# Two experts' feed-forward products put into the drain of an attention and mixture-of-experts kernel

## The chip, the cores and the metric

The kernel runs on one core of a Trainium2 chip. The metric is the device time of one execution in microseconds, and the time before is the median of three runs. TensorE (PE) does the matrix products, VectorE (DVE), ScalarE (ACT) and GpSimd (POOL) the work on vectors, and SyncE (SP) issues the transfers. The profile is of one execution.

## What is computed

The input is 32 batches of 128 tokens of 128 numbers. Two attention stages with modulated linear layers come first, each batch by itself; then a mixture of 8 experts over all 4096 tokens:

```
x = x + attn(cond(x))                       # 16 heads, softmax over tokens
tok = cond2(x)                              # 16 heads of 8, mixes heads of one token, then a linear layer
logits = tok @ gate_w.T ; probs = softmax(logits)
top2_w, top2_idx = top_k(probs, 2)
cap = int(1.25 * T / E)                     # 640
keep = (bincount(top2_idx) <= cap)          # an expert chosen more often is dropped whole
y[t, e] = relu(tok @ W1[e] + b1[e]) @ W2[e] + b2[e]
out = x + sum over e of (weight of e if chosen and kept) * y[t, e]
```

For the inputs of the reference the experts 0 to 7 are chosen 146, 280, 2077, 2615, 289, 1995, 572 and 218 times. Five of them (0, 1, 4, 6, 7) are at or below 640 and are kept. As first choices of the tokens of the first 24 batches they are chosen 20, 94, 928, 1247, 63, 521, 150 and 49 times.

## The kernel before

**The batch loop.** All engines walk through slots. Slot s works on batch s + 1 (queries, keys, values; stage A), s (scores and attention; B), s - 1 (output product, first residual, keys of the mixing stage; C), s - 2 (scores and softmax between heads; H) and s - 3 (the mixing sum and the last linear layer, whose result is one batch of `tok_all`; D). Slots -2 to 34 exist. From slot 32 (BATCH) on no attention is left: this is the drain. Each engine's order is the order in the text of its block; semaphores carry the dependences. In slots 33 and 34 `late(s)` puts the head scores first on DVE. The mixing sum of a batch is a product with the weights and a tree of adds: the first half of the shifts on DVE (`mix_lo`, L343 to L360), the other on POOL (`mix_hi`, L1056 and L1063); `mixed()` joins them. POOL also makes `pair` (L1068), the products from which DVE takes the head scores (L377); `score` is then completed by two copies on ACT (`head_copies`), and `weight` is the exponential on ACT (`head_weights`).

**Routing.** `gate_logits` on PE multiplies tiles of `tok_all` with the gate matrix. The tiles 0 to 27 (EARLY) come in six parts in slots 31 to 33 and one copy, the last four (RECENT) at the end. `first_choice` and `second_choice` on DVE pick the two best experts of each tile; then the count over all tokens (L434, a product with ones on PE, L753), `keep`, the gates, and a ranking that gives `order`, the kept experts first, and `n_run`, their number (L448 to L460). `step` makes each of these instructions wait for the one before. `keep_going(n)` on PE is n products of ones with no use for the result.

**The expert loop.** For each of the `n_run` experts, 8 quads of 4 tiles (512 tokens): `hidden` (L779, one product of 128x128 by 512 columns), `relu` on ACT into `hT`, `output` (L787, four products), and on DVE four instructions (L482) that add the result times the gate to `acc_all`. Each product in 32 bits appears in the profile as two instructions, so `hidden` is x2 and `output` x8. `acc_all` begins as the transposed x (`x1_transpose` on PE, `copy_x1` on ACT), to which the second bias is added (`bias_rows` L771 on PE, L470 on DVE). At an expert's start ACT loads its number from `order` and copies its weights (`set_expert`, `set_hidden`). In the last round SP writes each quad of `acc_all` out as it is done.

## Time and profile before

| | us |
|---|---|
| median of 3 runs (594.38 to 597.33) | 596.59 |
| profiled execution, its time | 596.94 |
| its span, first to last instruction | 595.1 |
| PE busy in the span | 575.1 (97%) |
| DVE busy | 483.7 (81%) |
| ACT busy | 372.0 (63%) |
| POOL busy | 288.1 (48%) |

Times inside the profile are microseconds from the span's start; 1.84 us of the execution lie outside its span. A busy PE is not a PE at its peak, since the ends of matmuls are modelled. The batch loop fills the span up to about 471 us, the drain and the routing go up to about 518 us, and the expert loop to the end.

### The profile page before, as it was taken

How to read it: one execution, taken by the hardware profiler on the slowest of the kernel's cores; microseconds unless marked ns; L12 is line 12 of the kernel's file. 1: busy time of each engine (PE TensorE's matmuls, PEld its weight loads, DVE VectorE, ACT ScalarE, POOL GpSimd, SP SyncE). 2: the span in 40 equal slices, each digit the busy share in tenths (PEclk: the TensorE clock that was granted, in tenths of full speed). 3: DMA queues.
4: the chain of work that ended last, by engine and by line, in shares of the span. 5: the costliest groups of instructions: out<-in, count | busy, mean ns of one | idle time of the engine just before them, and what ended most of it. 6: DMA issues, size and time to landing. Idle time of an engine off the chain costs nothing. (4 is left out here: it accounts for less than half of the span.)

```text
span 595.1 us, 15251 instructions
## 1 busy us (share of the span) xinstructions
PE 575.1 (97%) x4516; PEld 492.3 (83%) x4516; DVE 483.7 (81%) x1026; ACT 372.0 (63%) x855; POOL 288.1 (48%) x248
## 2 busy tenths in 40 slices
PE   8999999999999999999999999999998997799998
PEld 8888888888888888888888888888887896466775
DVE  4235888898989898988889898989898788777776
ACT  1767767777777677777777767777775321534443
POOL 1011666666666666666666666666666563000000
PEclk9999999999999999999999999999999977999999
DMA  7300000000000000000000000000000000000004
GB/s 240 86 2 2 1 3 2 0 0 0 0 0 0 0 0 0 0 0 0 0 0 0 0 0 0 0 0 0 0 0 2 1 1 0 1 1 0 0 0 141
DMA packets 9364, 7.18 MB, mean 12 GB/s; under 512 B 1089, under 2 KB 8833, under 8 KB 9217
## 3 DMA queue, kind: packets, MB, share of 16 engines
q1 hardware_dynamic: 9344, 6.94, 3.9%
q8 instruction: 11, 0.18, 0.1%
q14 instruction: 9, 0.07, 0.0%
HBM read 4.84 MB, written 2.10 MB: 12 GB/s over the span
## 5 line engine op out<-in xcount | busy, mean ns | idle before, releaser
L1068 POOL TENSOR_TENSOR pair<-kx 128x1152 f32<-128x1152 f32 x32 | 82.2, 2568 | 167.4 <-DVE shifted L388 158.4
L580 PE MATMUL bank_a<-v,prob 128*128 128x65 f32 x1024 | 128.5, 274 | 1.5 <-ACT prob L814 0.8
L580 PEld LDWEIGHTS bank_a<-v,prob 128*128 128x128 f32 x1024 | 121.8, 192 | 6.3 <-ACT prob L814 3.2
L1063 POOL TENSOR_TENSOR mix_hi<-mix_hi 128x512 f32<-128x512 f32 (+2 forms) x96 | 116.8, 1217 | 7.5
L271 DVE TENSOR_REDUCE row_max<-bank_s 128x4 bf16<-128x512 f32 x128 | 88.9, 694 | 26.2 <-PE bank_s L555 25.3
L814 ACT ACTIVATE prob<-bank_t 128x512 f32<-128x512 f32 x128 | 68.9, 589 | 6.9 <-PE bank_t L570 4.7
L587 PE MATMUL misc<-yT,wq_sb 128*128 128x128 f32 x512 | 69.6, 279 | 0.5 <-DVE yT L419 0.5
L570 PE MATMUL bank_t<-qT,kT 64*128 64x256 f32 x512 | 65.7, 376 | 0.0
L1056 POOL TENSOR_TENSOR mix_hi<-weight,kx 128x1024 f32<-128x1024 f32 x32 | 64.1, 2002 | 3.1 <-ACT weight L814 3.1
L282 DVE TENSOR_TENSOR att<-bank_a,recip_den 128x256 f32<-128x256 f32 x128 | 54.4, 425 | 13.0
L587 PEld LDWEIGHTS misc<-yT,wq_sb 128*128 128x128 f32 x512 | 62.0, 191 | 3.6 <-DVE yT L419 0.7
L814 ACT ACTIVATE attT<-misc 128x512 f32<-128x512 f32 x64 | 38.1, 595 | 42.1 <-PE misc L594 42.1
L660 PE MATMUL misc<-attT,wpost_sb 128*128 128x128 f32 x512 | 64.1, 278 | 0.0
L660 PEld LDWEIGHTS misc<-attT,wpost_sb 128*128 128x128 f32 x512 | 59.7, 192 | 0.0
L814 ACT ACTIVATE hT<-bank_t,b_now 128x512 f32<-128x512 f32 x42 | 28.9, 687 | 42.7 <-PE bank_t L779 42.6
L570 PEld LDWEIGHTS bank_t<-qT,kT 64*128 64x128 f32 x512 | 49.3, 189 | 4.9
L349 DVE TENSOR_TENSOR mix_lo<-mix_lo 128x512 f32<-128x512 f32 x32 | 52.4, 1637 | 1.1
L814 ACT ACTIVATE qT<-misc 128x512 f32<-128x512 f32 x64 | 38.0, 594 | 23.0 <-PE misc L587 23.0
L555 PE MATMUL bank_s<-k,q 128*128 128x256 bf16 x256 | 49.8, 276 | 1.9 <-ACT k L814 0.3
L343 DVE TENSOR_TENSOR mix_lo<-weight,kx 128x1024 f32<-128x1024 f32 x32 | 49.9, 1560 | 0.0
L779 PE MATMUL bank_t<-tok_all,w_now 128*128 (+1 forms) x84 | 42.1, 595 | 1.6 <-ACT w_now L814 1.6
L377 DVE TENSOR_REDUCE score<-pair 128x144 f32<-128x1152 f32 x32 | 43.1, 1346 | 0.0
(149 smaller groups left out, 998.9 us busy)
## 6 DMA issues: line engine op xcount, KB each, us to landing
...
b_rows<-in_b SPq DMA_DIRECT2D x16, 4.0 KB
```

The costliest lines, as they stand in the source:

```text
L271: V.tensor_reduce(bass.AP(row_max, first_w * (P + 1) + HPG * p, [[HPG * P, P], [P + 1, 2], [KEY, 2], [1, 1]]), bank_s[:, :, :].rearrange(" ...
L282: V.tensor_tensor(att[:, HPG * g:HPG * (g + 1), :], att_bank(g)[:, :, 0:KEY], recip_den[:, g % 2, :].unsqueeze(2).to_broadcast([P, HPG, KEY]),
L343: V.tensor_tensor(mix_lo[:, :, :].rearrange("p r (h e) -> p r h e", e=MD), weight[:, jd, 0:MH // 2, :].unsqueeze(3).to_broadcast([P, MH // ...
L349: V.tensor_tensor(mix_lo[:, 0:4, :], mix_lo[:, 0:4, :], mix_lo[:, 4:8, :], ALU.add).then_inc(s_lo, 1)
L570: last = mm(bank_t[half][:, w:w + 2, :], kT[rows, j, p, :], qT[rows, j, p, w:w + 2, :], start=False, stop=True, skip_group_check=True)
L580: last = mm(att_bank(g)[:, w, :], prob[:, g % 2, w, :], v1[:, j, g, :], start=(w == 0), stop=True, skip_group_check=True)
L587: last = mm(bank[:, c % 4, :], wq_sb[:, c * P:(c + 1) * P], yT[:, :], start=(c % 4 == 0), stop=True, skip_group_check=True)
L660: last = mm(misc[2][:, 0, :], wpost_sb[:, k, :], attT[:, k, :], start=(k == 0), stop=(k == CHUNKS - 1))
L814: return nc.scalar.activation(out_, in_, func, **kw)
L1056: G.tensor_tensor(mix_hi[:, :, :].rearrange("p r (h e) -> p r h e", e=MD), weight[:, jd, MH // 2:MH, :].unsqueeze(3).to_broadcast([P, MH / ...
L1063: G.tensor_tensor(mix_hi[:, 0:r, :], mix_hi[:, 0:r, :], mix_hi[:, r:2 * r, :], ALU.add).then_inc(s_hi, 1)
L1068: G.tensor_tensor(pair[:, :, :], bass.AP(kx2, jc * 2 * P, [[4 * P, P], [0, SHIFTS], [1, P]]), bass.AP(kx2, jc * 2 * P, [[4 * P, P], [MD, S ...
```

## The change

Two experts are computed ahead, in the drain, before it is known how many are kept. The first choices of the tokens of 24 batches are counted (`count_ahead`, with one product of ones on PE), and the two least chosen experts (`pick_ahead`) go into `ahead_order`. Their 16 units (an expert and a quad each) of `hidden`, `relu`, `output` and a copy to `ahead_out` (`ahead_keep`) are laid into slots 32 to 34 and behind them on PE and ACT, in place of most of `keep_going`; `unit` puts quad 7, which needs the last tokens, last. The loop then runs over the kept experts without these two (`not_ahead`, `keep_loop`), at least three times. With the counts above the two are experts 0 and 7, and 1, 4 and 6 are left. `ahead_out` is scaled with the gates and added to `acc_all` during the loop: 48 tiles are scaled by ACT, three behind each `relu` of the first two experts (`scale_three`), 16 by POOL, which also does all adding.

The other edits: the 24 early tiles' logits come in four parts in slot 31; the last eight are RECENT, and `second_choice` runs once over all 32. In the drain DVE makes the copies of `score` itself (`own_copies`), and the tree of adds of `mix_lo` is one strided reduction into `mix_part`. `mix_hi` has two buffers. The ranking for the loop goes ahead of the scaling of the gates. The transposes of x come behind the units, and the second half of them, the transposes of the gates and the bias products behind the first `hidden` products; the bias is added within the first expert. The loops of the first two experts are written out.

```
+AHEAD = 2
+EARLY, RECENT = range(BATCH - 2 * QUAD), range(BATCH - 2 * QUAD, BATCH)
...
+        UNITS = AHEAD * QUADS
+        HALF = QUADS // 2
+        SCALED = [(x, t) for q in range(QUADS) for x in range(1 if q < HALF else AHEAD)
+                  for t in range(q * QUAD, (q + 1) * QUAD)]
...
+            def ranked(into):
...
+            def count_ahead():
+
+                dve.wait_ge(s_log_mm, 4)
+                dve.wait_ge(s_const, 3)
+                top, fi = part(r_max, EARLY), part(first, EARLY)
+                lg = misc[0][:, :, :].rearrange("p w f -> p (w f)")[:, 0:len(EARLY) * EXPERTS].rearrange(
+                    "p (t e) -> p t e", e=EXPERTS)
+                step(V.tensor_reduce(top, lg, AX.X, ALU.max))
+                ROUTE_STEPS["tops"] = step(V.tensor_tensor(fi, lg, over_e(top), ALU.is_ge))
+                ROUTE_STEPS["count1"] = step(V.tensor_reduce(count[:, :], fi.rearrange("p t e -> p e t"), AX.X, ALU.add))
...
+            def pick_ahead():
+
+                dve.wait_ge(s_cnt1_mm, 1)
+                step(V.scalar_tensor_tensor(out=key[:, :], in0=bank_s[:, 0, 0:EXPERTS], scalar=float(EXPERTS),
+                                            in1=index8[:, :], op0=ALU.mult, op1=ALU.add))
+                ROUTE_STEPS["pick"] = ranked(ahead_order)
+                step(V.tensor_scalar(not_ahead[:, :], place[:, :], float(AHEAD), None, ALU.is_ge))
...
+                def drain_slot():
+                    def weight_sums():
+                        dve.wait_ge(s_weight, n(d))
+                        need(dve, s_mix, n(d - 1))
...
+                    if s == BATCH:
+                        count_ahead()
+                        weight_sums()
+                        pick_ahead()
...
+                    head_scores()
+                    own_copies()
+                    head_shift()
...
+                        V.tensor_reduce(mix_part[:, :], mix_lo[:, :, :].rearrange("p r f -> p f r"), AX.X,
+                                        ALU.add).then_inc(s_lo, 3)
+                        mixed(mix_part[:, :])
...
-            second_choice(RECENT, 2)
+            second_choice(range(BATCH), 2)
...
+            step(V.tensor_tensor(keep_loop[:, :], keep[:, :], not_ahead[:, :], ALU.mult))
+            step(V.scalar_tensor_tensor(out=key[:, :], in0=keep_loop[:, :], scalar=-float(EXPERTS), in1=index8[:, :],
+                                        op0=ALU.mult, op1=ALU.add))
+            ROUTE_STEPS["order"] = ranked(order)
...
+            ROUTE_STEPS["loop"] = step(V.tensor_tensor(loop_gates[:, :, :], gates[:, :, :], over_t(not_ahead), ALU.mult))
...
+            for q in range(QUADS):
+                dve.wait_ge(s_x1n, q + 1)
+                add_expert(0, q)
+                for done in ((q,) if q < HALF else (2 * q - 8, 2 * q - 7) if q >= QUADS - 2 else ()):
+                    add_b2(done)
             dve.wait_ge(s_b2, QUADS)
-            with dve.Fori(0, runs) as k:
+            for q in range(QUADS):
+                if q < HALF:
+                    dve.wait_ge(s_added, q + 1)
+                add_expert(1, q)
+            with dve.Fori(2, runs) as k:
...
-            early_ends = (0, 6, 10, 15, 20, 24, len(EARLY))
-            parts_early = [EARLY[a:b] for a, b in zip(early_ends, early_ends[1:])]
+            parts_early = [EARLY[a:b] for a, b in ((0, 6), (6, 13), (13, 19), (19, 24))]
...
+            def ahead_hidden(u):
+
+                x, q = unit(u)
+                need(pe, s_ah, u - 1)
+                if q == QUADS - 1:
+                    pe.wait_ge(s_tok, BATCH)
+                pe.wait_ge(s_ah_w1, x + 1)
+                mm(bank_t[u % 2][:, :, :], ahead_w1[:, x, :], tok_all[:, q * QUAD * P:(q + 1) * QUAD * P],
+                   start=True, stop=True).then_inc(s_ah_mm, 1)
+
+            def ahead_output(u):
+
+                x, q = unit(u)
+                pe.wait_ge(s_ah, u + 1)
+                need(pe, s_ao, u - 1)
+                for t in range(QUAD):
+                    last = mm(bank_a[u % 2][:, t * P:(t + 1) * P], hT[:, u % 2, t * P:(t + 1) * P],
+                              w2_sb[:, bass.ds(picked[x], 1), :].rearrange("p a f -> p (a f)"),
+                              start=(t == 0), stop=True, skip_group_check=True)
+                last.then_inc(s_ao_mm, 1)
...
+            def ahead(*units):
+
+                for u in units:
+                    ahead_output(u)
+                    if u + 2 < UNITS:
+                        ahead_hidden(u + 2)
...
+                if s_is(s, BATCH - 1):
+                    gate_logits(parts_early[0])
...
+                    keep_going(6)
+                    pick()
+                    pe.wait_ge(s_ld_ffn, 16 * (3 + P // EXPERTS))
+                    ahead_hidden(0)
...
+                    if s_is(s, BATCH):
+                        ahead(0, 1, 2)
                     if s_is(s, BATCH + 1):
-                        keep_going(40)
+                        ahead(4, 5, 6)
                     if s_is(s, BATCH + 2):
-                        keep_going(12)
+                        ahead(8)
+                        gate_logits(RECENT[:-1])
                     need(pe, s_tok, d)
                     pe.wait_ge(s_mix, n(d))
                     nc.tensor.transpose(misc[2][:, 0, :], mix[:, :], ident[:, :]).then_inc(s_mixT_mm, 1)
                 if s_is(s, BATCH):
-                    gate_logits(parts_early[5])
+                    ahead(3)
+                if s_is(s, BATCH + 1):
+                    ahead(7)
+                if s_is(s, BATCH + 2):
+                    ahead_output(9)
...
-            x1_transpose(range(QUADS // 2, QUADS))
+            ahead(12, 13, 14, 15)
+            x1_transpose(range(HALF))
...
+            x1_transpose(range(HALF, QUADS))
+            pe.wait_ge(s_rt, ROUTE_STEPS["gates"])
+            pe.wait_ge(s_x1n, QUADS)
+            for i in range(2):
+                src = gates[:, i * 16:(i + 1) * 16, :].rearrange("p t e -> p (t e)")
+                last = nc.tensor.transpose(misc[1][:, i, :], src, ident[:, :])
+            last.then_inc(s_gT_mm, 1)
+            for q in range(QUADS):
+                output(0, q, q % 2)
+                if q + 2 < QUADS:
+                    hidden(q + 2, q % 2)
+                if q == 0:
+                    pe.wait_ge(s_gT, 1)
+                    bias_rows(range(HALF))
+                if q == 5:
+                    bias_rows(range(HALF, QUADS))
...
+                def drain_slot():
+                    if s == BATCH:
+                        copy_att(c, 0)
+                        copy_att(c, 1)
+                        copy_logits(EARLY, 4)
+                        act.wait_ge(s_ld_ffn, 16 * (3 + P // EXPERTS))
+                        act.wait_ge(s_rt, ROUTE_STEPS["pick"])
+                        take_expert(0)
+                        x1_scaled()
+                        take_expert(1)
+                        ahead_relu(0)
+                        keys_out()
+                        ahead_relu(1)
+                        keys_twice()
+                        head_weights()
+                        ahead(0, 1, 2)
+                        mixing_out()
+                        ahead(3)
+                        tokens_out()
+                    if s == BATCH + 1:
+                        ahead(4)
+                        head_weights()
+                        ahead(5, 6)
+                        mixing_out()
+                        ahead(7)
+                        tokens_out()
+                    if s == BATCH + 2:
+                        ahead(8)
+                        mixing_out()
+                        ahead_keep(9)
+                        tokens_out()
+                        ahead_relu(11)
+                        copy_logits(RECENT, 6)
+                        route_exp(EARLY)
+                        route_exp(RECENT)
+                        ahead(10, 11)
...
+            def scale_three(i):
+
+                for x, t in SCALED[3 * i:3 * i + 3]:
+                    f(ahead_out[:, x, t, :], ahead_out[:, x, t, :],
+                      scale=ahead_gate[:, x, t:t + 1]).then_inc(s_scaled, 1)
...
+            for k in range(2):
+                e = next_expert(k)
+                for q in range(2, QUADS + 2):
+                    if q == QUADS:
+                        next_hidden(k, e)
+                    relu(k * QUADS + q + 1, q % 2)
+                    scale_three(k * QUADS + q - 2)
...
+            pool.wait_ge(s_ah_gate, AHEAD)
+            pool.wait_ge(s_ao, UNITS)
+            for q in range(QUADS):
+                quad = slice(q * QUAD, (q + 1) * QUAD)
+                own = q < HALF
+                if own:
+                    G.tensor_tensor(ahead_out[:, 1, quad, :], ahead_out[:, 1, quad, :],
+                                    ahead_gate[:, 1, quad].unsqueeze(2).to_broadcast([P, QUAD, P]),
+                                    ALU.mult).then_inc(s_pool_step, 1)
+                    pool.wait_ge(s_pool_step, 2 * q + 1)
+                pool.wait_ge(s_scaled, scaled_by(q))
+                G.tensor_tensor(ahead_out[:, 0, quad, :], ahead_out[:, 0, quad, :], ahead_out[:, 1, quad, :],
+                                ALU.add).then_inc(s_pool_step, 1)
+                pool.wait_ge(s_pool_step, 2 * q + 2 if own else HALF + q + 1)
+                pool.wait_ge(s_b2, q + 1)
+                pool.wait_ge(s_e, (2 if own else 2 + QUADS) * QUAD + QUAD * (q + 1))
+                G.tensor_tensor(acc_all[:, quad, :], acc_all[:, quad, :], ahead_out[:, 0, quad, :],
+                                ALU.add).then_inc(s_added, 1)
...
```

PE in the drain, from the last key transpose of slot 32 on. Before, slots 32 and 33, where L704 and L720 are the two products that end a batch's mixing stage and L526 is `keep_going`:

```order
L704 MATMUL misc2<-ident,mix 128x128
L610 MATMUL bank_s<-gate_sb,tok_all 128x8 x4
L720 MATMUL misc2<-mixT,modw_sb 128x128
L526 MATMUL bank_a1<-ones 128x128 x40
L704 MATMUL misc2<-ident,mix 128x128
L526 MATMUL bank_a1<-ones 128x128 x3
L720 MATMUL misc2<-mixT,modw_sb 128x128
```

And now, where L763 is `ahead_output`, L754 `ahead_hidden`, and L865 the former L704:

```order
L754 MATMUL bank_t1<-tok_all,ahead_w1 128x512
L852 MATMUL misc1<-ident,kxT 128x128
L763 ISA
L763 MATMUL bank_a0<-w2_sb,hT 128x128 x4
L754 MATMUL bank_t0<-tok_all,ahead_w1 128x512
L763 MATMUL bank_a1<-w2_sb,hT 128x128 x4
L754 MATMUL bank_t1<-tok_all,ahead_w1 128x512
L763 MATMUL bank_a0<-w2_sb,hT 128x128 x4
L754 MATMUL bank_t0<-tok_all,ahead_w1 128x512
L865 MATMUL misc2<-ident,mix 128x128
L763 MATMUL bank_a1<-w2_sb,hT 128x128 x4
L754 MATMUL bank_t1<-tok_all,ahead_w1 128x512
```

The filling products behind slot 32 are gone, and units stand ahead of and between the two products of each mixing stage.

PE behind the count of all tokens. Before:

```order
L753 MATMUL misc0<-count,ones 128x8
L621 MATMUL bank_t0<-ident,x_all 128x128 x4
L621 MATMUL bank_t1<-ident,x_all 128x128 x4
L621 MATMUL bank_a0<-ident,x_all 128x128 x4
L621 MATMUL bank_a1<-ident,x_all 128x128 x4
L759 MATMUL misc1<-ident,gates 128x128 x2
L771 MATMUL bank_a0<-b2_rows,gatesT 128x512
L771 MATMUL bank_a1<-b2_rows,gatesT 128x512
```

And now, where L916 is the count, L736 the transposes of x and L946 the load of `n_run` that stands ahead of the loop's first `hidden`:

```order
L916 MATMUL misc0<-count,ones 128x8
L763 MATMUL bank_a0<-w2_sb,hT 128x128 x4
L754 MATMUL bank_t0<-tok_all,ahead_w1 128x512
L763 MATMUL bank_a1<-w2_sb,hT 128x128 x4
L754 MATMUL bank_t1<-tok_all,ahead_w1 128x512
L763 MATMUL bank_a0<-w2_sb,hT 128x128 x4
L763 MATMUL bank_a1<-w2_sb,hT 128x128 x4
L736 MATMUL bank_a0<-ident,x_all 128x128 x4
L736 MATMUL bank_a1<-ident,x_all 128x128 x4
L736 MATMUL misc1<-ident,x_all 128x128 x4
L736 MATMUL bank_a0<-ident,x_all 128x128 x4
L946 TENSOR_LOAD n_run
```

Units 12 to 15 now stand between the count and the transposes of x, and the transposes ahead of the first `hidden` of the loop.

## Rows read from the trace of the kernel before

**Rows 1.** Page, costliest groups: relu of the loop.
```profile
L814 ACT ACTIVATE hT<-bank_t,b_now 128x512 f32<-128x512 f32 x42 | 28.9, 687 | 42.7 <-PE bank_t L779 42.6
```
**Rows 2.** Timeline, expert loop: start, duration, engine, line, out<-in, idle before.
```profile
518.09 1.16 PE L787 MATMUL bank_s<-w_run,hT 128*128 x8
...
526.32 1.05 PE L787 MATMUL bank_s<-w_run,hT 128*128 x8
...
527.80 1.30 DVE L482 SCALAR_TENSOR_TENSOR acc_all<-bank_s,gate_run,acc_all 128x128 f32 x4 [0.53 <-PE bank_s L787]
...
533.83 1.15 PE L787 MATMUL bank_s<-w_run,hT 128*128 x8
...
577.66 1.15 PE L787 MATMUL bank_s<-w_run,hT 128*128 x8
```
**Rows 3.** Timeline, slot 31, PE's waits and a part of the logits.
```profile
456.35 0.63 PE L594 MATMUL misc<-ident,att 128*128 128x128 f32 x4 [0.61 <-DVE att L282]
...
458.05 0.40 PE L652 MATMUL bank_s<-ident,row_max 128*128 128x128 bf16 x4 [0.79 <-DVE row_max L271]
...
460.12 1.40 PE L610 MATMUL bank_s<-gate_sb,tok_all 128*128 128x8 f32 x12
```
**Rows 4.** Windows of 3 us in the drain: busy time by engine, then granted clock.
```profile
474.00:477.00 3.00, 2.05 (x20) 1.96 (x19) 2.93 (x6) 0.40 (x1) 2.84 (x3) 1.00 0.00 0
...
480.00:483.00 3.00, 3.00 (x16) 3.00 (x16) 2.41 (x4) 1.17 (x4) 1.73 (x1) 0.50 0.00 0
...
492.00:495.00 3.00, 0.97 (x7) 0.81 (x7) 2.85 (x5) 0.42 (x1) 1.96 (x1) 1.00 0.00 0
```
**Rows 5.** Timeline, drain: DVE's share of the mixing, and what follows it.
```profile
482.11 2.81 DVE L343 TENSOR_TENSOR mix_lo<-weight,kx 128x1024 f32<-128x1024 f32 x1
...
489.36 1.34 DVE L377 TENSOR_REDUCE score<-pair 128x144 f32<-128x1152 f32 x1
...
492.48 0.42 ACT L814 ACTIVATE weight<-shifted 128x256 f32<-128x256 f32 x1 [1.11 <-DVE shifted L388]
...
497.93 1.21 DVE L343 TENSOR_TENSOR mix_lo<-weight,kx 128x1024 f32<-128x1024 f32 x1
...
504.15 0.46 ACT L814 ACTIVATE tok_all<-misc,modb_sb,demod 128x128 f32<-128x128 f32 x1 [0.58 <-PE misc L720]
```
**Rows 6.** Timeline, routing: transposes, copies, count, ranking, bias.
```profile
505.81 1.04 PE L621 MATMUL bank_a<-ident,x_all 128*128 128x128 f32 x8
...
506.92 1.09 ACT L814 ACTIVATE acc_all<-bank_a 128x512 f32<-128x512 f32 x2
...
508.07 0.61 DVE L434 TENSOR_REDUCE count<-chosen 128x8 f32<-128x256 f32 x1
...
511.14 0.17 DVE L448 SCALAR_TENSOR_TENSOR key<-keep,index 128x8 f32<-128x8 f32 x1
...
512.11 0.70 PE L771 MATMUL bank_a<-b_rows,gatesT 32*128 32x512 f32 x2 [0.51 <-ACT gatesT L814]
...
513.22 0.15 DVE L460 TENSOR_SCALAR n_run<-kept 128x1 int32<-128x1 f32 x1
...
514.33 0.20 ACT L814 ACTIVATE b_now<-b_sb 128x1 f32 x1 [2.28 <-DVE n_run L460]
...
514.50 1.28 DVE L470 TENSOR_TENSOR acc_all<-acc_all,bank_a 128x512 f32<-128x512 f32 x2 [0.90 <-issue]
```
**Rows 7.** Groups by shape, POOL from 494 to 498 us: a sum of 512.
```profile
L1063 POOL TENSOR_TENSOR mix_hi<-mix_hi 128x512 f32<-128x512 f32 x1 | 1.3, 1292 | 0.1
```
**Rows 8.** Groups by shape, whole span: the same sum, and ACT scaling one tile.
```profile
L1063 POOL TENSOR_TENSOR mix_hi<-mix_hi 128x512 f32<-128x512 f32 x32 | 67.1, 2096 | 2.5
...
L814 ACT ACTIVATE x1s<-x_all,style 128x128 f32 x26 | 10.4, 402 | 30.8 <-DVE x_all L353 30.8
```
**Rows 9.** Timeline, slot 31: POOL's sums and a DVE addition from PSUM.
```profile
457.90 4.07 POOL L1063 TENSOR_TENSOR mix_hi<-mix_hi 128x512 f32<-128x512 f32 x3
...
460.72 0.28 DVE L353 TENSOR_TENSOR x_all<-misc,x_all 128x128 f32<-128x128 f32 x1
```

416 lines of the change are left out of this document (250 added, 166 removed).

## The prediction

> **What bounds the kernel now.** I read the page first: relu runs 42 times [rows 1]. Two of these stand ahead of the expert loop and eight are in each round, so the loop has (42 - 2) / 8 = 5 rounds, as many as there are kept experts. Then the timeline of the loop. The first output product starts at 518.09 and that of the second expert at 533.83, a first round of 15.74 us; by the row at 577.66 the next three take (577.66 - 533.83) / 3 = 14.61 us each [rows 2]. PE sets this pace: a quad takes 14.61 / 8 = 1.83 us, and in it DVE works 1.30 us, then waits for PE, and ACT 0.69 us [rows 1, 2]. So five rounds are 15.74 + 4 x 14.61 = 74.2 us, up to 592.3, and 2.8 us follow.
>
> The stretch from about 471 to 518.09 is the other half of the matter. Here the engines take turns: the share of PE's time in use was 0.97 of 3 us in the window at 492, and its clock fell to the lower level, 1.2 GHz (granted 0.50), in that at 480, soon after a window (474) with 2.05 of 3 us busy [rows 4]. What sets the time there is a chain by way of DVE and POOL: head scores, weights of the last batch (492.48), mixing sum, its tokens (done 504.61), then the routing on DVE up to `n_run` (513.37) and ACT's load of the first expert's number (514.33) [rows 5, 6]. PE has room there, filled with products of ones.
>
> **Rounds taken out.** The two experts picked are 0 and 7 by the counts, both kept, so the loop makes max(3, 3) = 3 rounds. Two rounds go: -29.2 us. The rest of the sum is what this costs.
>
> **Slot 31.** All 24 early tiles' logits now stand here; 6 tiles take 1.40 us, 0.23 us each [rows 3]. Six of them enter where PE waited 0.61 us, +0.8; seven where it waited 0.79 us for `row_max`, +0.8; six stand where six stood, and five instead of four make 0.2. Behind those waits everything of the slot follows, so I count it whole: +1.7 us. Slot 32 loses its 18 tiles, but there PE had waits.
>
> **Slot 32.** DVE no longer starts with the sum of weights and products; it counts first (three steps, about 1.4 us), ranks (the same chain as from 511.14 to 513.37, 2.2 us [rows 6]) and only then adds x. Before, that addition was as late for another reason: the sums in `mix_lo` ran against POOL. So it stays near its time. The pick is ready about 4 us into the slot's DVE work; PE and ACT each load two numbers, for which the row at 514.33 gives about 1 us from the number to the first copy [rows 6]. These delay the key products by 1.2 us on PE and `kx` by 1.6 on ACT. Who waits: POOL's `pair` of batch 31. Before, it waited for `shifted` of batch 30 until 481.27; now `shifted` comes at about 478.9 (no mixing ahead of it) and `kx` at 480.4, so `pair` starts 0.8 us earlier than before. The first `ahead_output` starts at about 479.8.
>
> **The mixing sum.** The three adds of `mix_lo` become one reduction. The nearest row below is the reduction of 1152 numbers, 1.34 us, read in another order; a reduction with a stride took 0.61 us for 256, which for 1024 gives 1.9 us at most by proportion above a fixed 0.15 [rows 5, 6]. I take 1.5. What it gives is mainly a place free of POOL: the product ahead of it took 2.81 us beside POOL and 1.21 us alone [rows 5]. The Trainium skill (SBUF — State Buffer, section "Who interferes with whom") says that a DVE reduction never contends with GpSimd, while a DVE instruction with two SBUF inputs does; the two rows of the product agree, and by it the reduction would cost its own time only. With head scores first in every slot, batch 31 goes so: `pair` 2.6 us from 480.4, the reduction 1.34, its copies, maximum and shift some 1.7, so shifted at 486.1; ACT takes it behind unit 6's relu, its weights at 490.4 (before 492.90). POOL's product and three sums (about 2.0 and 2.7 us, the largest sum 1.29 [rows 7]) and the join follow, some waits between them, and the sum of batch 31 is ready at about 497.3.
>
> **The drain by PE.** From 479.8 to the tokens of batch 31 PE has ten outputs and nine hiddens ahead of them, 9.5 x 1.83 = 17.4 us, seven tiles of logits 1.7, five small products of the mixing 1.9, and then the last product's hop over ACT, PE and ACT, 1.5: 502.3. The mixing sum at 497.3 is earlier than PE gets to it, so PE is the bound here, and its clock counts. The trace had the lower level for about 7 us from 478 on behind such a half-filled slot 32 [rows 4]; slot 32 is filled no better now. Work of 3 us is lost if it comes again; I take 2.5. With slot 31 the tokens are at 502.3 + 1.7 + 2.5 = 506.5, 1.9 later than the 504.61 of before.
>
> **Routing.** From tokens to the end of the count it was 508.68 - 504.61 = 4.1 us [rows 5, 6]. Now `second_choice` is 256 wide instead of 32, seven steps at about 0.45 instead of 0.22, +1.6, and the copy of the logits stands behind a relu, +0.7: 6.3 us, so 512.8. The product over it 0.5: 513.3. PE has idled some 2.5 us by then. Ranking comes 2 us earlier after the count than before, but nobody waits for that now: PE first does units 12 to 15, four outputs and two hiddens, 5.7 us: 519.0. The last copy 0.7; then four quads of transposes (0.52 each) and, slower, their copies on ACT (0.55 each [rows 6]), 2.7: 522.4. ACT loads the number and copies `w1`, 0.8; two hiddens 1.9: 525.1; the other four quads with their copies 3.0; the transposes of the gates 0.5. The loop's first output is at **528.6, against 518.09: +10.5 us**.
>
> **The three rounds.** The first holds eight bias products in two lots. One takes 0.70 us [rows 6]; four side by side use different rows of the array, and I take 1.2 a lot (0.7 to 2.8): +2.4. DVE has 8 x 1.30 and 8 x 0.64 (from the row of two at 514.50 [rows 6]), 15.5 us, less than the round. ACT has a relu of 0.69 and three tiles to scale: 0.40 us each alone [rows 8], less back to back, as two copies in 1.09 show; 0.8 to 1.2 for three against the 1.83 of a quad. So 0 to 0.1 us a quad, and I take 0.5 us a round for the borders, where ACT also loads and copies weights. POOL makes 20 sums of 512, 1.29 us each by the nearest row [rows 7]: 26 us of the 32 in two rounds, and each quad of the first four (3.9 us) is due only in the second round. Hidden. Rounds: 14.6 + 2.4 + 0.5 = 17.5, 15.1, 14.6: 47.2 us. End of the loop 575.8, the same 2.8 us of tail: span 578.6.
>
> **The sum.** Span before 595.1, now 578.6, -16.5. With the 1.84 us outside the span, 580.4 against the profiled 596.94; the median is 0.35 lower, so **580 us**.
>
> **Rivals.**
> - The clock stays up in the drain, since units take the place of waits: no 2.5 us, and scaling on ACT costs nothing, 1.0 less: 576.5. For: PE is filled from 479.8 on. Against: what came before the fall at 478 stays. 20%.
> - The clock falls twice, the second time in the 2.5 us of idle ahead of the count, as after the window at 492: another 3.5 us of lost work, 583.5 to 587 where slot 32 takes longer too. 17%.
> - POOL is late. Beside DVE its sum took 2.10 us in the mean of 32 [rows 8]. A first quad is then 6.4 us, four 25.7, and the fourth is due at the second round's fourth quad, 17.5 + 5.5 = 23 us in: DVE waits about 3, and again somewhat in the third round: 584. 8%.
> - Slower: DVE's additions in the loop (L482) share POOL's port and wait out each sum. The row at 460.72 speaks against it: an addition from PSUM took its 0.28 us in the midst of POOL's sums [rows 9]. But L482 also reads a gate from SBUF. If each of 20 sums at 1.29 to 2.10 us holds DVE, its 20.8 + 5.1 us in two rounds become 52 to 68 instead of 32.6: 599 to 615. It decides from about 1.2 us lost a sum. 4%. The Trainium skill's same section lets a DVE instruction with one SBUF input outside the fast modes pass POOL; by that the price is zero.
> - The change doesn't do what it says: a picked expert is not kept. With one, four rounds, 594.6; the counts (146 and 218 against 640) exclude it but for an error of mine. 1%.
>
> My forecast has 50%. The range takes in both clock cases, the late POOL, and the bounds above: 574 to 588. About 0.5% is what a measurement can tell from no change: faster 0.94, same 0.02, slower 0.04.
>
> **What would show it.** relu of the loop 26 times, and 16 units; first output of the loop near 528.6; three rounds of 17.5, 15.1 and 14.6 us; `mix_part` at 1.2 to 1.9 us whatever POOL does; L482 at its 0.33 us a tile beside POOL's sums; POOL ready before the third round. A window at granted 0.50 after 478 would show the clock term. Wrong would be a first output after 535 or DVE waiting for `added`.

## The result and the profile after

| | before | after |
|---|---|---|
| median, us | 596.57 (594.38 to 597.33, 4 runs) | 577.02 (574.82 to 579.19, 4 runs) |
| ratio to before | | 0.9678, 95% interval 0.9622 to 0.9734 |
| profiled execution, its time | 596.94 | 579.19 |
| its span | 595.1 | 577.4 |

The change takes off 19.6 us. The page of after gives the busy time of each engine, and the chain by engine:

```profile
PE 559.4 (97%) x4408; PEld 475.4 (82%) x4408; DVE 457.8 (79%) x966; ACT 390.7 (68%) x911; POOL 310.5 (54%) x268
...
PE 81%; DVE 8%; ACT 5%; issue 3%; DVEq 1%; POOL 0%; ACTq 0%; POOLq 0%
```

PE is as full as before, 97%, with 15.7 us less to do. The loop now has three rounds, as the output products that begin them show, in the timeline of PE (start, duration, then engine, line and operation):

```profile
527.30 1.06 PE L939 MATMUL bank_s<-w_run,hT 128*128 128x128 f32 x8
...
544.18 1.15 PE L939 MATMUL bank_s<-w_run,hT 128*128 x8 [0.17 <-DVE acc_all L569]
...
559.05 1.15 PE L939 MATMUL bank_s<-w_run,hT 128*128 x8 [0.17 <-issue]
```

The first round begins at 527.30, where it was 518.09 [rows 2]: 9.2 us later. The rounds take 16.88 and 14.87 us, and 18.35 go from the third round's start to the end of the span. Between slot 32 and the loop this is what stands at the places the sum spoke of, in the timeline of all engines:

```profile
478.41 0.31 ACT L985 ACTIVATE ahead_w<-w_sb 128x128 f32 x1 [3.48 <-DVE not_ahead L384]
...
481.43 0.33 PE L852 MATMUL misc<-ident,kxT 128*128 128x128 f32 x1
481.65 1.15 PE L763 MATMUL bank_a<-w_sb,hT 128*128 x8
482.17 1.92 DVE L514 TENSOR_REDUCE mix_part<-mix_lo 128x128 f32<-128x1024 f32 x1
...
484.17 0.38 ACT L985 ACTIVATE kx<-misc 128x256 f32<-128x256 f32 x1 [2.16 <-DVE mix_part L514]
...
484.63 2.59 POOL L1346 TENSOR_TENSOR pair<-kx 128x1152 f32<-128x1152 f32 x1 [7.73 <-ACT kx L985]
...
485.98 1.16 PE L763 MATMUL bank_a<-w_sb,hT 128*128 x8 [0.56 <-ACT hT L985]
...
492.46 0.41 ACT L985 ACTIVATE weight<-shifted 128x256 f32<-128x256 f32 x1
...
495.15 1.25 DVE L398 TENSOR_TENSOR mix<-mix_sum,h_rden 128x128 f32<-128x128 f32 x1
...
496.55 0.30 PE L865 MATMUL misc<-ident,mix 128*128 128x128 f32 x1 [1.21 <-DVE mix L398]
...
503.98 0.45 ACT L985 ACTIVATE tok_all<-misc,modb_sb,demod 128x128 f32<-128x128 f32 x1
...
509.96 0.61 DVE L533 TENSOR_REDUCE count<-chosen 128x8 f32<-128x256 f32 x1
...
510.72 0.36 PE L916 MATMUL misc<-count,ones 128*128 128x8 f32 x2 [2.24 <-DVE count L533]
...
519.06 1.06 PE L736 MATMUL bank_a<-ident,x_all 128*128 128x128 f32 x8 [0.78 <-ACT ahead_out L985]
```

Two things in it are not as in the sum. ACT's copy `kx` of batch 31 waits 2.16 us for DVE's `mix_part` of batch 29, a wait for the buffer: `kx2` has two halves, and batch 31 is to be written to the one of batch 29. What reads that half is DVE's product, and it was done at 482.07; but the copy's wait counts up to the end of the reduction behind it (484.09), which reads only `mix_lo`. And unlike before [rows 4], the clock falls not in the drain's middle but at its two ends, as the windows show (busy time of PE, PEld, DVE, ACT and POOL, then the granted clock):

```profile
465.00:468.00 3.00, 3.00 (x26) 2.74 (x27) 1.22 (x4) 0.67 (x3) 0.00 (x0) 0.88 0.00 0
468.00:471.00 3.00, 3.00 (x15) 1.92 (x13) 1.01 (x2) 1.78 (x6) 1.29 (x1) 0.55 0.02 5
...
480.00:483.00 3.00, 2.85 (x15) 1.74 (x14) 2.86 (x4) 1.67 (x3) 0.00 (x0) 1.00 0.00 0
...
507.00:510.00 3.00, 1.48 (x8) 0.65 (x6) 2.76 (x8) 1.74 (x3) 0.00 (x0) 1.00 0.00 0
510.00:513.00 3.00, 2.28 (x12) 1.79 (x12) 2.57 (x10) 0.60 (x1) 0.00 (x0) 0.78 0.00 0
513.00:516.00 3.00, 3.00 (x12) 2.19 (x11) 2.69 (x10) 1.16 (x2) 0.00 (x0) 0.66 0.00 0
```

The second fall follows the 2.24 us in which PE waits for the count, as one of the rivals had it. The first stands at the end of slot 31, behind windows in which PE was busy (2.73 of 3 us at 462, 3.00 before).

### The profile page after: what moved, and what is told of

Same layout as the page of the kernel before. It is cut to its first block, busy times and chain, and to the rows that moved or that the text cites. A ratio compares the mean times of both kernels' runs of the same rounds, so it can differ in the third digit from the quotient of the medians.

```text
span 577.4 us, 14607 instructions
## 1 busy us (share of the span) xinstructions
PE 559.4 (97%) x4408; PEld 475.4 (82%) x4408; DVE 457.8 (79%) x966; ACT 390.7 (68%) x911; POOL 310.5 (54%) x268
## 4 chain that ended last, share of the span: by engine, by line
PE 81%; DVE 8%; ACT 5%; issue 3%; DVEq 1%; POOL 0%; ACTq 0%; POOLq 0%
PE bank_a L692 18%; PE misc L699 10%; PE misc L815 10%; PE bank_t L682 8%; PE bank_s L667 6%; PE misc L706 5%; PE misc L833 3%; PE bank_t L677 3%; PE bank_t L931 3%; PE misc L835 2%; DVE row_max L296 2%; DVE h_max L412 2%; PE bank_s L939 2%; PE misc L939 2%; PE bank_s L807 1%
## 5 line engine op out<-in xcount | busy, mean ns | idle before, releaser
L450 DVE TENSOR_TENSOR mix_lo<-mix_lo 128x512 f32<-128x512 f32 x29 | 47.2, 1627 | 1.0
L444 DVE TENSOR_TENSOR mix_lo<-weight,kx 128x1024 f32<-128x1024 f32 x29 | 43.8, 1511 | 0.0
L985 ACT ACTIVATE q<-qT 128x512 bf16<-128x512 f32 x64 | 40.3, 630 | 1.1
L706 PE MATMUL misc<-ident,att 128*128 128x128 f32 x256 | 39.2, 276 | 0.5 <-DVE att L307 0.5
```

The source lines that it names most:

```text
L706: last = nc.tensor.transpose(misc[1 + half][:, c % 4, :], att[:, 2 * c:2 * c + 2, :].rearrange("p h e -> p (h e)"), ident[:, :])
L985: return nc.scalar.activation(out_, in_, func, **kw)
```

## The experiments

Each is compared with the kernel before on its own chip, and changes the kernel after unless said otherwise. The changed kernel again, the last units first, the keys' own buffer and the tree ran on one chip (before: 598.18 us). So did, later, the long filling and the two runs with the count product between the units (598.23). Nothing combined, one expert ahead, both together and the drain's order alone ran on a second (598.29), the shorter filling on a third (597.9). Between chips it is the ratio to before that can be compared. The theory at the start: the two rounds out are worth what a round takes, and the rest is PE's chain through the drain, in which a wait for `kx`, the strided sum, the place of the last four units and the combining each have a price of their own. The rivals: units are nearly free, or the drain's new order on DVE and ACT brings a good part of it.

**The changed kernel again.**

> The changed kernel again, as the base of the others on the same chip. My theory of its spread (575.0 to 579.2 us in four runs): TensorE's clock falls to its lower level once or twice around the drain, and each fall costs 1 to 2 us, so runs lie in two groups. The rival, a spread of the batch loop itself, would show in the time at which slot 32 begins. Expected: median 575 to 579 us, and in the profile one or two stretches with a granted clock near 0.5 to 0.7.

578.23 us (577.35 to 583.32), ratio 0.9686 (0.9656 to 0.9715). In this profile the clock did not fall anywhere between 450 and 531, so the one or two stretches expected there did not come; its fall stands at 9 to 15 us (granted 0.83 and 0.60). The first output came at 525.97, and the two rounds took 16.89 and 14.86 us. The time does go with the mean granted clock. Of the ten executions of this kernel two at 1.0 took 574.8 and 575.0 us, four at 0.996 to 0.997 577.4 to 578.2, three at 0.993 579.0 to 579.3, and one at 0.985 583.3.

The rival, a spread of the batch loop, is half right. From the first transposes of `att` to those of slot 31 the fourteen profiles, that of before too, take 421.4 to 421.6 us: the loop is steady. But the first ones start anywhere from 31.06 to 34.17 us. Up to 3 us between two profiles thus stand ahead of everything that an edit has touched, so two profiles are compared below from slot 31 or from a later common place. What makes the start differ was not followed.

The repeated run is the yardstick for what follows, and for slot 31. The first transposes of `att` in that slot stand at 455.48 (454.92 before), and the second ones of slot 32 at 473.00:

```profile
455.48 0.60 PE L706 MATMUL misc<-ident,att 128*128 128x128 f32 x4
...
473.00 0.63 PE L706 MATMUL misc<-ident,att 128*128 128x128 f32 x4 [0.45 <-DVE att L307]
```

Before, they were at 471.28. The lag grows from 0.56 to 1.72 us, so all of slot 31's new logits cost 1.2 us.

**The last units ahead of the count.**

```
             pe.wait_ge(s_log, 2)
+            ahead(12, 13, 14, 15)
             pe.wait_ge(s_rt, ROUTE_STEPS["count"])
             mm(misc[0][:, 0, 0:EXPERTS], ones[:, :], count[:, :], start=True, stop=True).then_inc(s_cnt_mm, 1)
-            ahead(12, 13, 14, 15)
             x1_transpose(range(HALF))
```

> Units 12 to 15 stand ahead of the count of all tokens instead of behind it. Theory: behind the drain PE is the bound, and it idles 2.2 us ahead of the count and then has 5.3 us of units in front of the transposes; taken first, the units fill the idle time, and the ranking, later by about 3 us, is still ready when ACT has copied the transposes: 2 to 3.5 us faster than the changed kernel, the loop's first output near 524.5. Rival: the ranking on DVE and ACT's load of the expert's number set the start of the loop; then the count's delay of 3.3 us goes straight through and it is 1 to 3 us slower.

574.97 us (573.83 to 575.35), ratio 0.9604 (0.9587 to 0.9622): 3.3 us less than the changed kernel by the medians, with intervals that do not overlap. From the tokens of batch 31 to the first output the profile has 19.06 us (504.41 to 523.47), against 21.66 in the repeated run (504.31 to 525.97): 2.6 us. In PE's timeline the wait for the count is gone, and the one for the first weights stays (1.24 us, 1.15 in the repeated run):

```profile
512.25 2.10 PE L763 MATMUL bank_a<-w_sb,hT 128*128 x16
514.19 0.29 PE L917 MATMUL misc<-count,ones 128*128 128x8 f32 x2
515.13 1.07 PE L736 MATMUL bank_a<-ident,x_all 128*128 128x128 f32 x8 [0.66 <-ACT ahead_out L985]
...
518.34 1.98 PE L931 MATMUL bank_t<-tok_all,w_now 128*128 128x512 f32 x4 [1.24 <-ACT w_now L985]
```

From 504 to 513 its windows hold 3.00 of 3 us of PE at granted 1.00. So the place of the four units was wrong by some 3 us: work that does not need the count stood behind the wait for it.

**A buffer of its own for the keys of batch 31.**

```
-        kx2 = sb("kx2", [P, 2, 2 * P])
+        kx2 = sb("kx2", [P, 3, 2 * P])
...
+                kc, kd = (2 if s_is(c, BATCH - 1) else jc), (2 if s_is(d, BATCH - 1) else jd)
...
-                    need(act, s_lo, 4 * n(c - 2))
-                    need(act, s_hi, 4 * n(c - 2))
-                    f(kx2[:, jc, :].rearrange("p (r f) -> p r f", r=2),
+                    if kc != 2:
+                        need(act, s_lo, 4 * n(c - 2))
+                        need(act, s_hi, 4 * n(c - 2))
+                    f(kx2[:, kc, :].rearrange("p (r f) -> p r f", r=2),
```

> The last batch's keys (kx) get a buffer of their own, so that ACT's copy of them in slot 32 no longer waits for the mixing of batch 29 on DVE (2.2 us). Theory: this wait, which I had not seen, also holds ACT's relu of unit 2 and PE behind it, and POOL's pair; without it the copy comes at about 482.0 instead of 484.2, PE's waits ahead of units 2 and 5 (1.4 and 2.0 us) shrink, and the last tokens come 1 to 2 us earlier: 1 to 2 us faster. Rival: the mixing of batches 30 and 31 on DVE is the bound of the drain, which does not start earlier: within 0.5 us of the changed kernel.

577.35 us (576.88 to 577.60), ratio 0.9652 (0.9635 to 0.9668). That is 0.9 us less than the repeated run by the medians, but the intervals of the ratios overlap.

```profile
453.21 0.61 PE L707 MATMUL misc<-ident,att 128*128 128x128 f32 x4
...
480.67 0.38 ACT L986 ACTIVATE kx<-misc 128x256 f32<-128x256 f32 x1
...
481.12 2.59 POOL L1350 TENSOR_TENSOR pair<-kx 128x1152 f32<-128x1152 f32 x1 [5.47 <-ACT kx L986]
...
502.21 0.45 ACT L986 ACTIVATE tok_all<-misc,modb_sb,demod 128x128 f32<-128x128 f32 x1
...
508.95 0.36 PE L917 MATMUL misc<-count,ones 128*128 128x8 f32 x2 [2.24 <-DVE count L534]
```

`kx` waits for nothing, and `pair` starts at 481.12. The tokens of batch 31 begin at 502.21 against 504.31 in the repeated run, but 2.1 us is not what the buffer gives. This execution was already 2.27 us ahead at the start of slot 31 (453.21 against 455.48). From there its tokens take 49.00 us. The repeated run, whose clock did not fall on the way, takes 48.83, and the first profile of the changed kernel, whose clock fell near the same place as here (granted 0.59 and 0.84 at 465 and 468), takes 49.34 (454.64 to 503.98). Against its like the buffer is worth 0.3 us at the tokens, and 0.4 at the loop's first output (72.25 against 72.66 us from slot 31). PE waits the same 2.24 us for the count, and here too the clock falls behind it (window in the same columns as above):

```profile
510.00:513.00 3.00, 3.00 (x10) 1.97 (x10) 2.60 (x12) 1.28 (x2) 0.00 (x0) 0.50 0.00 0
```

So the wait for the key buffer is real, and hardly anything hangs on it: what goes is PE's wait of 0.56 us ahead of unit 2, while the one of 1.2 us for `mix` stays (1.22 at 494.78). That is the rival's case, within 0.5 us, and not the theory's 1 to 2.

**The tree of adds instead of the strided reduction.**

```
-                        V.tensor_reduce(mix_part[:, :], mix_lo[:, :, :].rearrange("p r f -> p f r"), AX.X,
-                                        ALU.add).then_inc(s_lo, 3)
-                        mixed(mix_part[:, :])
+                        for i, r in enumerate((4, 2, 1)):
+                            V.tensor_tensor(mix_lo[:, 0:r, :], mix_lo[:, 0:r, :], mix_lo[:, r:2 * r, :],
+                                            ALU.add).then_inc(s_lo, 1)
+                            if r > 1:
+                                dve.wait_ge(s_lo, 4 * d + i + 2)
+                        mixed(mix_lo[:, 0, :])
```

> In the drain the strided reduction of mix_lo is again the tree of three adds. The reduction measures 1.92 to 1.96 us, the tree alone 0.69 + 0.38 + 0.29 = 1.36 us, but up to 4.4 us beside POOL. Theory: in slots 33 and 34 the tree runs beside POOL's product and sums, is longer by 0 to 2 us in each, and holds POOL's sums up as well: 0 to 2 us slower, at the last tokens. Rival: as the two now take turns otherwise, the tree is 0.6 us shorter in each slot, up to 1.5 us faster.

581.87 us (580.10 to 582.83), ratio 0.9722 (0.9703 to 0.9740): 3.6 us more, beyond both the theory (0 to 2) and the rival. The three adds of slot 32, of slot 33 and what followed them:

```profile
482.84 1.48 DVE L515 TENSOR_TENSOR mix_lo<-mix_lo 128x512 f32<-128x512 f32 x3
...
492.94 4.20 DVE L515 TENSOR_TENSOR mix_lo<-mix_lo 128x512 f32<-128x512 f32 x3
...
498.62 0.30 PE L868 MATMUL misc<-ident,mix 128*128 128x128 f32 x1 [3.04 <-DVE mix L398]
```

Alone the tree takes 1.48 us, less than the 1.92 of the reduction. Beside POOL's product and sums (493.18 to 498.32) it takes 4.20, where the reduction took 1.96 beside the product, PE waits 3.04 us instead of 1.21, and behind that the clock is at 0.64 and 0.79 in the windows of 498 and 501. The reduction in slot 33 is what decides; in slots 32 and 34 the tree is 0.4 us quicker (1.48 us in both). How the 3.6 us divide between the longer wait and the clock behind it is not shown.

**Nothing combined.**

```
-                    scale_three(k * QUADS + q - 2)
...
-                if q < HALF:
-                    dve.wait_ge(s_added, q + 1)
...
-                        dve.wait_ge(s_added, q + i + 1)
...
-            for q in range(QUADS):
-                quad = slice(q * QUAD, (q + 1) * QUAD)
...
-                G.tensor_tensor(acc_all[:, quad, :], acc_all[:, quad, :], ahead_out[:, 0, quad, :],
-                                ALU.add).then_inc(s_added, 1)
```

> The results of the two experts computed ahead are neither scaled (48 tiles on ACT, 16 on POOL) nor added (POOL's 16 sums) to the output; all else stays, so their part is missing from what comes out. Theory: the combining lies beside PE's work and costs only where ACT's scaling and its loads meet at the border of an expert: 0 to 1.5 us faster than the changed kernel (577 to 578 us). Rival: POOL's sums hold DVE's additions or the loop waits for them: 4 us faster or more, and DVE's 0.28 us a tile would fall.

This kernel leaves the two experts' part out of its output. 576.74 us (574.22 to 579.70), ratio 0.9662 (0.9641 to 0.9683), some 1.5 us less than the changed kernel, on another chip and with intervals that overlap. In the profiles the first two rounds take 16.88 and 14.67 us (16.88 and 14.87 after). The difference lies in the last round, DVE's timeline there:

```profile
563.60 1.30 DVE L591 SCALAR_TENSOR_TENSOR acc_all<-bank_s,gate_run,acc_all 128x128 f32 x4 [0.73 <-issue]
564.98 1.30 DVE L591 SCALAR_TENSOR_TENSOR acc_all<-misc,gate_run,acc_all 128x128 f32 x4
```

and the same two quads of after, where DVE waits for `added` ahead of each quad:

```profile
564.67 1.30 DVE L594 SCALAR_TENSOR_TENSOR acc_all<-bank_s,gate_run,acc_all 128x128 f32 x4 [0.71 <-issue]
566.13 1.42 DVE L594 SCALAR_TENSOR_TENSOR acc_all<-misc,gate_run,acc_all 128x128 f32 x4 [0.16 <-issue]
```

With the combining two quads take DVE 3.57 us (564.67 to 568.24), without it 3.41 (563.60 to 567.01), and PE needs 3.50. So with it DVE sets the pace of the last round: from the round's first output to DVE's last addition it is 15.62 us after, 15.06 without combining, 14.76 before. The run takes out the wait instruction, ACT's scaling and POOL's sums together, so it does not show which of them costs the 0.16 us.

**One expert ahead.**

```
-AHEAD = 2
+AHEAD = 1
...
-                        ahead(4, 5, 6)
+                        ahead(4)
+                        ahead_output(5)
+                        ahead_output(6)
+                        pe.wait_ge(s_ao, 7)
+                        keep_going(12)
                     if s_is(s, BATCH + 2):
-                        ahead(8)
+                        keep_going(12)
                         gate_logits(RECENT[:-1])
...
-            ahead(12, 13, 14, 15)
```

> Only one expert (0) is computed ahead: 8 units instead of 16, the loop has four rounds, some products of ones fill PE where units were. Theory: a round costs 14.6 us in the loop; in the drain the last four units behind the count cost 5.3 us with the 0.8 us wait for their last copy, the others lie beside the chain by way of DVE and cost up to 2 us. So one expert ahead is 14.6 - 6 to 8 = 7 to 9 us slower than two, 584 to 587 us, and the first expert alone is worth 11 to 14 us. Rival 1: units in the drain are free: 13 us or more slower than two (590 us or more). Rival 2: PE is the bound all through the drain: each unit costs its 1.75 us and one is as good as two (577 to 580 us).

591.33 us (589.73 to 591.40), ratio 0.9884 (0.9867 to 0.9901). The second expert is worth 13.1 us by the medians (11.8 by the ratios, since the repeated run has one execution of 583.32), nearly its whole round of 14.6. By this run alone its units are nearly free, as the first rival had it. But the tokens of batch 31 begin at 503.86 here and at 504.31 with 16 units (49.1 and 48.8 us from the start of slot 31), and the windows behind them are unlike:

```profile
504.00:507.00 3.00, 2.03 (x5) 1.11 (x5) 0.00 (x0) 1.20 (x4) 0.00 (x0) 0.63 0.00 0
507.00:510.00 3.00, 1.94 (x8) 1.64 (x8) 2.70 (x9) 1.03 (x3) 0.00 (x0) 0.50 0.00 0
510.00:513.00 3.00, 0.72 (x4) 0.76 (x5) 2.46 (x7) 0.00 (x0) 0.00 (x0) 0.50 0.00 0
```

PE waits 3.34 us for the count and is at the lower clock up to 522; the first four `hidden` instructions of the loop take 3.78 us instead of 1.98. Were the units free, or did they keep up the clock? Two more runs asked that.

**One expert ahead, PE's waits filled.** On top of the edit for one expert; `fill(n)` is `keep_going(n)` into a bank that nobody reads.

```
+                if s_is(s, BATCH + 1) or s_is(s, BATCH + 2):
+                    fill(5)
                 if D:
                     pe.wait_ge(s_mixT, n(d))
...
                 if s_is(s, BATCH + 2):
+                    fill(6)
                     ahead_hidden(7)
                     gate_logits(RECENT[-1:])
+                    fill(5)
                     ahead_output(7)
+                    fill(32)
```

> One expert ahead, as in the run with one, but PE's idle places in slots 33 and 34 and ahead of the count product are filled with products of ones into a bank that nothing reads (5 + 5 + 6 + 5 + 32 of them). In the run with one expert (591.33) PE idled 3.34 us ahead of the count product and its granted clock was 0.50 to 0.63 from 504 to 522. Theory: a good part of the 13 us between one and two experts ahead is the clock, which the units of the second expert keep up; with the filling it stays at 1.00 up to the loop, the four hidden and transposed tiles there go at full speed, and the time is 587.5 to 589.5. Rival: the units are simply nearly free places for 14.6 us of loop, and the clock's part is small: 590.5 to 592, as before, or more where the filling delays the count product.

592.02 us (591.66 to 593.56), ratio 0.9908 (0.9880 to 0.9935). The clock stayed at 1.00 from 471 to 531, and the time is no better, since the filling was too long:

```profile
509.11 7.31 PE L643 MATMUL bank_s<-ones 128*128 128x128 f32 x64
```

The 32 products took 7.31 us, up to 516.4, with the count ready at 513.1 (512.47 and 0.62). A product takes 7.31 / 32 = 0.23 us. By itself the run settles nothing. So once more, with 2, 2, 3, 2 and 16 products:

**One expert ahead, filled less.**

> As the filled run with one expert ahead (592.02), with less filling: 2, 2, 3, 2 and 16 products of ones instead of 5, 5, 6, 5 and 32. There the clock stayed at 1.00 and the first output came 5.4 us behind the first weights of the loop, against 7.4 in the run with one expert and no filling; but the filling, 7.31 us for the 32, held the count product about 3.3 us, and the tokens about 1. Theory: without that delay the clock's part is seen by itself: the first output of the loop 2 to 3 us earlier than 524.57, the time 588 to 590 against 591.33. Rival: the clock's part is nothing on the whole, since the low clock falls on stretches in which PE waits for DVE and ACT anyway: 590.5 to 592.

587.55 us (586.31 to 589.36), ratio 0.9834 (0.9812 to 0.9857): 3.8 us less than without filling by the medians, from 25 products whose result nobody reads. The two ran on different chips; the ratios to before differ by 3.0 us, with an interval of some 1.3 to 4.7.

```profile
508.06 3.74 PE L643 MATMUL bank_s<-ones 128*128 128x128 f32 x32
512.47 0.36 PE L926 MATMUL misc<-count,ones 128*128 128x8 f32 x2 [0.67 <-DVE count L533]
516.72 1.99 PE L940 MATMUL bank_t<-tok_all,w_now 128*128 128x512 f32 x4 [2.06 <-ACT w_now L994]
```

The granted clock is 1.00 from 474 to the loop. The first output comes at 521.77 against 524.57, 2.8 us earlier, though the tokens are 0.8 later, as this execution's start was. From tokens to first output it is 17.14 us against 20.71: 3.6 us. Since the filling does no work, this rules out that the low clock costs nothing. Against one expert with PE kept busy, the second is worth 587.55 - 578.23 = 9.3 us by the medians, and 10.4 by the profiles, from the first transposes of `att` to the end (552.5 and 542.1 us). So its eight units cost some 4 to 5 us of the 14.6, and 3 to 4 of the 13.1 are the clock, which the units keep up.

**The count ahead and the third buffer together.**

```
+            ahead(12, 13, 14, 15)
             pe.wait_ge(s_rt, ROUTE_STEPS["count"])
...
+        kx2 = sb("kx2", [P, 3, 2 * P])
```

> The keys' own buffer and the units ahead of the count together. Theory: the two gains add, since the tokens come about 2 us earlier (measured with the buffer alone, where a fall of the clock ahead of the count took half of it back) and no idle time is left ahead of the count: 5 us faster than the changed kernel, about 572 to 573 us. Rival: with the units ahead of the count ACT's load or the gates become the bound, and it is no faster than the units ahead alone, 575 us.

574.66 us (574.52 to 579.63), ratio 0.9614 (0.9599 to 0.9628): no better than the units first alone, 574.97 (0.9604), as the rival said. The third buffer adds nothing, which fits the 0.3 to 0.4 us read above.

**The count product between the units.** It stands behind unit 13, ahead of 14:

```
             pe.wait_ge(s_log, 2)
+            ahead(12, 13)
             pe.wait_ge(s_rt, ROUTE_STEPS["count"])
             mm(misc[0][:, 0, 0:EXPERTS], ones[:, :], count[:, :], start=True, stop=True).then_inc(s_cnt_mm, 1)
-            ahead(12, 13, 14, 15)
+            ahead(14, 15)
```

> The count product stands between unit 13 and unit 14 on PE, instead of ahead of 12 or behind 15. In the run with the units first (574.97) the count was ready at about 510.5, PE reached its product at about 513.3, and PE later waited 0.66 us for a copy and 1.24 us for the first expert's weights in the loop. Theory: the count product meets a count that is ready, n_run comes some 3 us sooner, the 1.24 us go, and the clock stays up: 573.5 to 574.3. Rival: PE gets there before the count is ready and waits again, the clock falls as in the changed kernel, 576 to 578.

575.19 us (572.55 to 575.76), ratio 0.9609 (0.9578 to 0.9639), the same as with all four units first, and neither what the theory nor what the rival said. The count product came 1.9 us earlier (512.29 against 514.19), and nothing followed from it. ACT shows why:

```profile
514.97 0.15 DVE L544 TENSOR_SCALAR n_run<-kept 128x1 int32<-128x1 f32 x1
...
517.35 0.62 ACT L986 ACTIVATE acc_all<-bank_a 128x512 f32<-128x512 f32 x1
...
518.00 0.31 ACT L986 ACTIVATE w_now<-w_sb 128x128 f32 x1
```

`n_run` is there at 515.12, yet `w_now` stands behind ACT's four copies of x, the last of which ends at 517.97. With all four units first `n_run` came at 517.02 and `w_now` at 517.98, just as late. PE's wait for `w_now` is one for ACT's queue, not for the routing, and the theory's reading of it fell.

**The same with the third buffer.**

> The same with a third key buffer for batch 31, so that the tokens of batch 31 come some 2 us earlier. Theory: what the third buffer saved is not taken back by an idle PE, since two units lie ahead of the count product: 572 to 573.5. Rival: as with the units first and the third buffer (574.66), the time saved ahead of the tokens turns up as a wait behind them, or the clock falls: 574 to 576.

574.49 us (572.34 to 574.71), ratio 0.9607 (0.9583 to 0.9632): no clear gain over 0.9609 without the buffer, as the rival said. From the start of slot 31 the tokens of batch 31 take 48.64 us here (452.86 to 501.50) and 48.65 without it (455.80 to 504.45). The best that was found is the four versions with units ahead of the count, at 574.5 to 575.2 and ratios of 0.9604 to 0.9614. Three of them ran on the repeated run's chip and are 3 to 4 us below it.

**The drain's new order alone, in the kernel before.** Head scores and own copies first in the slots 32 to 34, the strided reduction, two halves of `mix_hi`; no expert ahead, five experts in the loop.

```
+        mix_part = sb("mix_part", [P, P])
+        mix_hi = sb("mix_hi", [P, 2, MH // 2, P])
...
+                    head_scores()
...
+                    head_shift()
...
+                    V.tensor_reduce(mix_part[:, :], mix_lo[:, :, :].rearrange("p r f -> p f r"), AX.X,
+                                    ALU.add).then_inc(s_lo, 3)
+                    mixed(mix_part[:, :])
```

> The kernel before, with the changed kernel's order of the mixing stage on DVE in slots 32 to 34 alone: x first, head scores, the copies of score on DVE, one strided sum; two buffers of mix_hi. No expert ahead. Theory: DVE no longer takes turns with POOL in product and adds, the last weights come several us earlier, and the last tokens 3 to 5 us: 592 to 595 us against 597 to 598. Rival: the fill of 40 products of ones in slot 33 and the clock set the drain's length: within 1.5 us of the kernel before. If it is faster, that much of the change's 19 us belongs to the order of the mixing and not to the experts ahead.

596.21 us (594.05 to 598.49, 12 runs), ratio 0.9973 (0.9960 to 0.9985), 2.1 us less than before by the medians and 1.6 by the ratio. The tokens of batch 31 begin at 502.85 there (504.15 before), and the first output at 517.32 (518.09); of this 0.3 us stands at the start of slot 31 already (454.61 against 454.92). Its clock fell too, with PE without work:

```profile
477.00:480.00 3.00, 0.00 (x0) 0.00 (x0) 2.83 (x6) 0.00 (x0) 0.00 (x0) 0.50 0.00 0
480.00:483.00 3.00, 0.54 (x4) 0.57 (x4) 2.19 (x3) 0.43 (x2) 0.85 (x1) 0.50 0.00 0
```

So the new order has a small gain of its own, about what the rival allowed (1.5) and short of the theory's 3 to 5. It is about a tenth of the change; whether it is worth the same with the experts ahead was not run.

## Why the prediction was right, step by step

580 us were forecast, 577.0 measured, and the span was forecast at 578.6 and came at 577.4. The mechanism was right: two rounds go, and the drain's work costs less than they gave. By its steps, where the prediction's times inside the drain get the 1.7 us that it adds for slot 31 at the end:

| | forecast | measured in the profile |
|---|---|---|
| slot 31's logits | +1.7 | +1.2 (repeated run; 2.4 here with the fall of the clock in it) |
| first `ahead_output` | 479.8 + 1.7 | 481.65 |
| `pair` of batch 31 | 480.5 + 1.7 | 484.63 |
| weights of batch 31, done | 490.4 + 1.7 | 492.87 |
| sum of batch 31, done | 497.3 + 1.7 | 501.43 |
| `mix_part` | 1.5 | 1.92, 1.96, 1.94 |
| first `ahead_output` to the tokens' end | 22.5, and clock 2.5 | 22.8 |
| tokens' end | 506.5 | 504.43 |
| tokens to count | 6.3 | 6.1 |
| units 12 to 15 | 5.7 | 7.2 |
| from there to the first output | 9.6 | 9.0 |
| first output of the loop | 528.6 | 527.30 |
| the rounds and the tail | 17.5, 15.1, 17.4 | 16.88, 14.87, 18.35 |

**Rounds taken out: right.** -29.2 us, and what it costs was forecast within 1.3 us.

**How much of the agreement is luck.** The table's misses are larger than what they leave. The tokens' end came 2.1 us earlier than forecast, units 12 to 15 took 1.5 longer, the stretch behind them 0.6 less, the two rounds 0.8 less, the tail 0.9 more: some 6 us of misses that add up to 1.2. The other 1.8 of the 3.0 us between 580 and 577.0 is that the profiled execution lay 2.2 above its median, where the sum took 0.35.

**The mixing sum: the chain was wrong, the end was not.** The step said that `kx` comes at 480.4 and `pair` with it. With slot 31 in it that is 482.1, and `pair` came at 484.63. Of these 2.4 us the 2.16 are the copy's wait for the sum of batch 29, which the new order puts behind the head scores of batch 30. I had looked at what holds `pair`, and not at what holds the buffer that `kx` is written to. The sum of batch 31 (`mix_part` at 498.78, `mix` done at 501.43) was then 2.4 us later than forecast, and still ahead of PE, which reached it at 502.25. That is why the error cost next to nothing: the step "PE is the bound here" held, with 0.56 and 1.21 us of waits in its way. The run with a buffer of its own puts the price at 0.3 us at the tokens, and the other two runs with it at nothing.

**The strided reduction: mis-sized, within its bounds.** 1.92 to 1.96 us, not 1.5; the proportion from the strided row gives 4 x 0.46 + 0.15 = 1.99, not quite the 1.9 that the text has [rows 6]. It does not feel POOL: 1.92 alone, 1.96 beside its product, where the tree took 1.48 and 4.20. The Trainium skill (SBUF — State Buffer, section "Who interferes with whom") has it so for reductions and for instructions with two SBUF inputs, and the rows agree. What the text overlooked is the small join behind the reduction: `mix`, with two SBUF inputs, took 1.25 us beside POOL's sums in slot 33 (495.15) and 0.29 in slot 34, and it is most of the 1.21 us that PE waited there.

**The clock: near in size, wrong in place.** 2.5 us were put behind a fall at about 478, by the likeness to before [rows 4]. There was none: the windows from 471 to 510 have 1.00. In the profiled run it fell at 465 to 471 and behind the wait for the count. The first fall costs 1.2 us at slot 32 (18.74 us from slot 31's transposes to 473.38, against 17.52 in the repeated run, which had none) and 0.5 at the tokens (49.34 against 48.83). The second makes units 12 to 15 take 7.2 us instead of the repeated run's 5.5. Together that is 2.2 us. The rival "clock stays up" was right for the drain's middle, the rival "falls twice" for the second fall, as a mechanism; neither gave the time. That 2.5 us suited the total is luck. The repeated run shows that the clock need not fall there at all, and the two executions at a mean granted clock of 1.0 took 574.8 and 575.0 us, where the sum without its clock term gives 577.5.

**The first output and the rounds: right.** Four bias products take 1.13 us a lot (529.15 to 530.28, in four rows of 0.70 and 0.59 side by side); I had taken 1.2. The 0.5 us a round for the borders was mostly too much in the first two. The last round was forecast as before and was 0.9 us longer; of this 0.56 goes with the combining (15.62 against 15.06). The prediction counted DVE's work there, 8 x 1.30, and put nothing between the quads, where the profile has pauses of 0.16 and 0.7 us as "issue". That the wait for `added` makes them longer is likely, and not shown by itself.

**The other rivals: out.** POOL is not late: its sums took 1.27 us, not 2.10. The last began 3.5 us into the third round and ended at 563.82. So POOL was not ready before the third round, as the prediction's signs had it, and it cost nothing: DVE came to that quad at 573.26.

```profile
533.35 1.12 DVE L569 SCALAR_TENSOR_TENSOR acc_all<-bank_s,gate_run,acc_all 128x128 f32<-128x128 f32 x4
...
562.55 1.27 POOL L1375 TENSOR_TENSOR acc_all<-acc_all,ahead_out 128x512 f32<-128x512 f32 x1
```

Nor does DVE wait for POOL's port: L569 (the former L482) took 1.12 us for four tiles while POOL's sum of 533.39 ran, less than the 1.30 of before [rows 2]. Both picked experts were kept: the loop has three rounds.

**The point that the prediction missed altogether** is one of order: units 12 to 15 need nothing of the count and stood behind it. "PE has idled some 2.5 us by then" stands in the text on record, and the conclusion was not drawn; the units placed first were worth 3.3 us, the largest single gain that was found.

What stays open: why the clock falls at 465 to 471 in some executions of the same kernel, behind windows in which PE was busy, and not in others; why the executions differ by up to 3 us in their first 34; and whether the kernel before loses time by its own two falls (granted 0.50 in the windows of 480 and of 498), which would be a part of the 19.6 us that no run separates.
